# One list of 128 sums per head for the ranks above 8, sums of squares on TensorE, and new orders of work

## The reference

```python
q = (hidden_states @ Wq.T + bq).reshape(b, s, H, QD)            # H 8, QD 64
q = (q - mean) / sqrt(var + 1e-5) * ln_g + ln_b
s0 = l2norm(q[..., :32]) . l2norm(keys0)                        # 64 scores
s1 = l2norm(q[..., 32:]) . l2norm(keys1)                        # 64 scores
sc0, ix0 = top_k(s0, 16); sc1, ix1 = top_k(s1, 16)
cs = sc0[..., :, None] + sc1[..., None, :]                      # 256 cells
ci = ix0[..., :, None] + ix1[..., None, :]
fs, pos = top_k(cs, 16);  fi = ci at pos;  w = softmax(fs)
out = sum over the 16 of  gelu(x . expert_down[fi]) * w * expert_up[fi]
```

## Time and profile before

| | us |
|---|---|
| median of 3 runs (1389.09 to 1393.25) | 1392.88 |
| the profiled execution | 1389.55 |
| its span, first to last instruction | 1387.7 |
| DVE busy, share of the span | 1284.9, 93% |
| PE busy | 1029.8, 74% |
| POOL busy | 940.4, 68% |
| ACT busy | 919.2, 66% |
| mean granted clock of TensorE | 0.759 |

### The profile page before, as it was taken

How to read it: one execution, slowest core, us unless ns; L and a number is a source line. 1 busy time by engine, 2 the same in 40 slices (tenths; PEclk the granted TensorE clock), 3 DMA queues, 4 the chain that set the end, 5 groups by cost and what they waited for, 6 DMA issues and landing times.

```text
span 1387.7 us, 41186 instructions
## 1 busy us (share of the span) xinstructions
PE 1029.8 (74%) x9585; PEld 679.4 (49%) x9585; DVE 1284.9 (93%) x10050; ACT 919.2 (66%) x4155; POOL 940.4 (68%) x1947
## 2 busy tenths in 40 slices
PE   4767777877777777778778777786778878776753
PEld 2434554645455454555446454553545545463433
DVE  4349999999999989999899998999999999999995
ACT  2576867668586857858576784767658676766532
POOL 4438776786867768577677867676776777668552
PEclk7787786769788776878877696787868778685555
DMA  2100000000000000000000000000000000000000
GB/s 55 18 15 2 3 11 3 4 8 6 10 4 11 4 5 11 4 10 4 12 4 5 9 6 10 4 12 3 5 9 5 6 3 5 4 4 5 3 4 7
DMA packets 22512, 10.97 MB, mean 8 GB/s; under 512 B 13920, under 2 KB 22032, under 8 KB 22242
## 3 DMA queue, kind: packets, MB, share of 16 engines
q1 hardware_dynamic: 21618, 7.79, 2.5%
q10 hardware_dynamic: 624, 0.30, 0.1%
HBM read 4.58 MB, written 3.01 MB: 5 GB/s over the span
## 4 chain that ended last, share of the span: by engine, by line
DVE 60%; issue 15%; PE 8%; ACT 7%; POOL 6%; SPq 1%; DVEq 1%; DMA 0%; POOLq 0%; ACTq 0%
DVE idx L1466 14%; DVE val L1464 9%; DVE cr L1536 8%; DVE scores L1469 8%; DVE oh L1479 6%; DVE best L1534 4%; DVE wl L1499 3%; ACT ns_junk L863 2%; PE banks L1055 2%; DVE bns L1389 2%; DVE masked L1419 1%; POOL cs L623 1%; PE bankM L1219 1%; PE bankQ L1142 1%; ACT act_g L840 1%
## 5 line engine op out<-in xcount | busy, mean ns | idle before, releaser
L1466 DVE FIND_INDEX8 idx<-val,scores 124x8 uint16<-124x64 f32 x1536 | 304.4, 216 | 0.0
L1464 DVE MAX8 val<-scores 124x8 f32<-124x64 f32 x1536 | 210.6, 207 | 2.4 <-ACT scores L870 1.2
L1219 PE MATMUL bankM<-wl,oh 128*128 128x16 f16 x5952 | 162.8, 172 | 46.2 <-DVE wl L1499 46.2
L1219 PEld LDWEIGHTS bankM<-wl,oh 128*128 128x128 f16 x5952 | 160.0, 101 | 59.6 <-DVE wl L1499 33.2
L597 POOL TENSOR_TENSOR qscale<-nmx,power 124x16 f32<-124x16 f32 x48 | 147.8, 3079 | 45.4 <-DVE nmx L1443 45.3
L1469 DVE MATCH_REPLACE8 scores<-val,scores 124x64 f32<-124x64 f32 x768 | 151.4, 206 | 0.0
L863 ACT ACTIVATE ns_junk<-bankQ 124x32 f32<-124x32 f32 x768 | 138.0, 255 | 12.7 <-PE bankQ L1172 12.4
L1479 DVE TENSOR_SCALAR oh<-eh 128x992 f16<-128x992 int16 x384 | 135.2, 414 | 4.5 <-ACT eh L918 4.5
L863 ACT ACTIVATION_READ_ACCUMULATOR ns_junk<-bankQ 124x1 f32 x768 | 138.3, 268 | 0.0
L1108 PE MATMUL banks<-diag,probs 124*124 124x124 f32 x672 | 107.7, 327 | 25.0 <-ACT diag L808 25.0
L1227 PE MATMUL bankM<-up_x,prod 128*124 128x128 f32 x384 | 86.5, 396 | 50.5 <-DVE prod L1508 50.5
(11 more groups left out here) (196 smaller groups left out, 3067.8 us busy)
## 6 DMA issues: line engine op xcount, KB each, us to landing
x_in<-in_x SPq DMA_DIRECT2D x16, 93.8 KB
x_in<-in_x SPq DMA_DIRECT2D x16, 62.5 KB
out<-o_sb SPq DMA_DIRECT2D x16, 62.0 KB
out<-o_sb SPq DMA_DIRECT2D x16, 61.0 KB
out<-o_sb SPq DMA_DIRECT2D x16, 60.5 KB
x_in<-in_x SPq DMA_DIRECT2D x16, 31.0 KB
oh<-more SPq DMA_DIRECT2D x6, 54.0 KB
conv_w<-in_L_tok_kernel ACTq DMA_DIRECT2D x2, 128.0 KB, 3.2
```

Of the source, the lines that this page charges most:

```text
L1219: last = e.matmul(coef[:, g, :, :], oh[:, k, g, :, :].rearrange("p v t -> p (v t)"), wl[:, part, k, :, TG * g:TG * (g + 1)], start=k + par ...
L1464: last = v.max(out=v_[:, hd, s, best8], in_=src[:, hd, s, :])
L1466: last = v.max_index(out=i_[:, hd, s, best8], in_max=v_[:, hd, s, best8], in_values=src[:, hd, s, :])
```

## The change

**Ranks.** Only the first 8 of each list are ranked (`rank` steps 0 and 1; `val`, `idx`, `val_s` are half as long). Then ScalarE "lifts" the two lists of a head in place (`lift`, 16 instructions of 124x64 in a tile): every score is scaled by its own `qscale` and the best value of the other half is added. The first 8 are struck out already, so both lists hold the sums of the cells with one rank above 7. `late` (DVE) takes MAX8 over the 128 sums of a head straight into the last 8 places of `cs`, and later FIND_INDEX8. Cells are 34 + 8 = 42 in place of 50. `index_floats` (ACT) has 5 instructions in place of 1 and part 2 of `rank_sums` (POOL) 4 more, to make a place among 128 into an expert number. `scores`, `val`, `idx`, `qscale` and others have three buffers, one for each t, in place of two.

**Queries.** Both query products are computed turned (4 groups of 128x124 in place of one of 124x512). ScalarE squares all in one instruction; `q_sums` and `q_half_sums` (PE, 4 matmuls each with the squares as weights) add over partitions. `q_var` (ACT) adds the epsilon, which POOL did. `q_guard` reads its sums from `bankQ`; `bankQ` is free only when that has run on DVE (`nmx_ready`).

**Orders.** The five lists are written anew.

```diff
-                    best8 = slice(0, 8) if step < 2 else slice(8, 16)
+            def late(c, t, half, step):
+                n = c.tile(t)
+                if step == 0:
+                    dve.wait_ge(lifted, 2 * n + 1 + half)
+                    wait(dve, exp_ready, n)
+                else:
+                    dve.wait_ge(late_ready, 4 * n + 2 * half + 1)
+                for hd in range(4 * half, 4 * half + 4):
+                    both = scores[c.ring(t)][:, hd, :, :].rearrange("p s e -> p (s e)")
+                    if step == 0:
+                        last = v.max(out=cs[:, hd, INNER:NC], in_=both)
+                    else:
+                        last = v.max_index(out=late_idx[c.ring(t)][:, hd, :], in_max=cs[:, hd, INNER:NC], in_values=both)
...
+            def lift(c, t, half):
+                act.wait_ge(vals_scaled, 2 * n + 1 + half)
+                act.wait_ge(ranked, 8 * n + 4 * (half + 1))
+                for hd in range(4 * half, 4 * half + 4):
+                    for s in range(2):
+                        one = scores[c.ring(t)][:, hd, s, :]
+                        last = a.activation(one, one, ACT.Identity, scale=qscale[c.ring(t)][:, hd, s:s + 1], bias=val_s[c.ring(t)][:, hd, 1 - s, 0:1])
+                last.then_inc(lifted, 1)
...
-                for i in range(2 * H):
-                    last = a.activation(ns_junk[:, i, :], bankQ[0:NT, i * HALF:(i + 1) * HALF], ACT.Square, accum_out=nss[:, i // 2, i % 2:i % 2 + 1])
-                last.then_inc(nss_ready, 1)
+                a.activation(sqT[:, :], bankQ[:, 0:PAIRS * NT], ACT.Square).then_inc(squared2, 1)
...
-                wait(pe, nss_ready, n)
+                wait(pe, nmx_ready, n)
...
+            def q_half_sums(c, t):
+                pe.wait_ge(squared2, n + 1)
+                for k in range(PAIRS):
+                    last = e.matmul(bankQ[0:NT, 4 * k:4 * k + 4], sqT[:, k * NT:(k + 1) * NT], blocks_sb[:, 2:6], start=True, stop=True)
```

More of the change, by code:

```diff
@@ L51, in merge_matrix @@
                 m[h * NC + CELLS.index(p), h * SLOTS + s] = 1
+    for k in range(LATE):
+        for h in range(2):
+            m[h * NC + INNER + k, h * SLOTS + SLOTS - LATE + k] = 1
     assert m.sum() == 2 * NC
@@ L846, in q_squares, with q_var @@
                 act.wait_ge(q_done, n + 1)
-                wait(act, std_ready, 5 * n - 4)
-                for i in range(H):
-                    last = a.activation(sq_junk[:, i, :], bankQ[0:NT, i * QD:(i + 1) * QD], ACT.Square, scale=QD ** -0.5, accum_out=qss[:, i:i + 1])
-                last.then_inc(qss_ready, 1)
+                a.activation(sqT[:, :], bankQ[:, 0:PAIRS * NT], ACT.Square, scale=QD ** -0.5).then_inc(squared, 1)
+            def q_var(c, t):
+                n = c.tile(t)
+                act.wait_ge(qsum_done, n + 1)
+                wait(act, std_ready, 4 * n)
+                a.activation(qvar[:, :], bankQ[0:NT, 0:H], ACT.Identity, bias=eps8[:, 0:1]).then_inc(qvar_ready, 1)
             def q_stdT(c, t):
@@ L957, in body @@
                 do(q_squares, c, 2)
+                do(weight_high, c, 0)
+                do(q_var, c, 2)
+                do(lift, c, 1, 0)
                 do(p1_ln, c + 1, 1)
@@ L993, in body @@
                 do(q_gelu, c + 1, 3)
+                do(p1_probs, c + 2, 0)
+                do(index_floats, c, 2)
+                do(q_squares, c + 1, 1)
+                do(p1_diag, c + 2, 0)
+                do(best_exps, c, 2)
+                if not at(c + 1, 0):
+                    do(q_scores, c + 1, 0)
+                do(mark, c, 2)
             run(act, start, body, lambda: None)
@@ L1139, in q_inner @@
                 if low == 0:
-                    pe.wait_ge(nss_ready, 3 * b + 1)
+                    pe.wait_ge(nmx_ready, 3 * b + 1)
                 wait(pe, gelu_done, EL * b + low)
@@ L1276, in body @@
                     do(q_score, c, 0)
+                do(q_product, c, 1)
                 do(p1_scores, c + 1, 1)
-                do(q_product, c, 1)
+                do(q_sums, c, 1)
                 do(p1_turn_attn, c + 1, 0)
@@ L1618, in body @@
                 do(p1_rden, c + 1, 1)
-                do(invert_sums, c + -1, 2)
+                do(product, c + -1, 1)
                 do(p1_smax, c + 1, 2)
                 if at(c, 0):
-                    for step in range(4):
+                    for step in range(2):
                         rank(c, 0, 1, step)
-                if not at(c, 0):
-                    do(rank, c, 0, 0, 2)
-                if not at(c, 0):
-                    do(rank, c, 0, 0, 3)
                 if not at(c, 0):
@@ L1668 @@
     given += [("merge", merge_matrix()), ("identity", np.eye(128, dtype=np.float32)),
-              ("own", np.tile(np.eye(TG, dtype=np.float32), (EH, 1)))]
+              ("own", np.tile(np.eye(TG, dtype=np.float32), (EH, 1))),
+              ("blocks", np.concatenate([np.kron(np.eye(k, dtype=np.float32), np.ones((128 // k, 1), np.float32)) for k in (2, 4)], 1))]
     for name, a in given:
```

375 lines of the change are left out of this document (210 added, 165 removed).

## The result

The changed kernel takes 1495.76 us (median of 4 runs, 1485.63 to 1499.87) against 1393.07 (4 runs, 1389.09 to 1394.31) of the kernel before. The ratio is 1.0732, with a 95% interval from 1.0667 to 1.0796: slower by 7%, where 1378 was forecast. The profiled execution has a span of 1489.9 us.

The account below looks back on a forecast made before the run. The prediction took VectorE, busy 93% of the span, as the bound. From 1389.55 us it took 84 saved, added 81 of waits and took 8 back: 1378, own range 1364 to 1386, whole range 1337 to 1413.

Parts of the forecast that it names:

- VectorE's work: VectorE's ranks and `choose`: net saving of 1.76 us a tile, 84 us over 48 tiles.
- The lift: ScalarE's lift instructions: 0.34 us each, 2.7 us a group of 8, 5.4 us a tile.
- The three waits: New waits on VectorE from the new order: together 5.8 us a batch, 81 us in the run.
- Point 1: VectorE's `p1_shift` of the first norm waits for POOL's two steps: 1.5 us a batch.
- Point 3: VectorE's `late` of tile 0's second half waits for its lifts on ScalarE: 1.8 us a batch.
- Point 2: VectorE's `late` step 0 of tile 2's second half waits for ScalarE's queue: 2.5 us a batch.
- The turned products: Query products on TensorE: turning them costs nothing or a few tenths of a us either way.
- The sums: Sums of squares on TensorE: 16 new matmuls a tile at 0.135 us, 2.2 us a tile.
- I cost it at nothing: `bankQ`'s chain with `q_guard`: ScalarE's 3 us a tile given back against 2.2 for sums, so no cost.
- The cover: VectorE, 93% busy, would hide TensorE's added work, TensorE going from 63 to about 70 us of 81.
- The slower rival: Tile 2's `q_var` comes late on ScalarE, delaying the norm: 2.5 us a batch, 35 over 1378, 1413; chance 0.25.
- what is taken in: Scattered idle time in VectorE's loop that the new waits would absorb: 8 us back.

Follow-up runs that it names:

- e8: Changed kernel with one-instruction lift per half, row-shaped query products and one matmul in place of four in each sum: 1371.29 us (0.986).
- e2: Changed kernel with only the two query products back in their old row shape: 1455.95 us (1.0456).
- e6: Changed kernel with one matmul in place of four in each of the two sums of squares: 1456.58 us (1.0458).
- e5: Changed kernel with one-instruction lift per half and row-shaped query products together: 1388.69 us (0.9983).
- e3: Changed kernel with the lift of a half in one constant-scale instruction in place of 8 with per-row operands: 1425.03 us (1.0244).
- e7: Kernel before with the query half of the change alone, ranks and orders otherwise as before: 1517.15 us (1.0906).
- e13: Kernel before with both query products done twice in tile 0 alone: 1440.27 us.
- e15: Kernel before with `q_score` done twice in every tile, query products once: 1395.48 us.
- e4: Changed kernel with the first norm's `p1_shift` moved behind `finish` and the first step of `rank`: 1493.28 us (1.0697).
- e11: Kernel before with both query products done twice in all tiles: 1454.25 us.
- e9: Kernel before with the query half of the change, and tile 0's `q_guard` moved five `rank` steps up: 1519.13 us (1.0916).

## Why the prediction was wrong, point by point

- **VectorE's work: right.** 71 us less against 84, and 82 less in e8; the rates over 128 elements are as forecast.
- **The lift: right.** 0.34 us each. ScalarE's busy time is 1031, 1070 was forecast.
- **The three waits: right in place, and in size as a sum.** Point 1 is 1.25 us a batch in place of 1.5. Point 3, tile 0's second half, is 2.48 in place of 1.8, with another 1.24 ahead of the first half in some bodies. Point 2 came out smaller, 0.7 to 1.4, since VectorE was itself held up by TensorE's `experts_out` just before. Together they added 89 us against 81; that the sum fits so well is in part luck, since point 2 came out at half its size and point 3 larger.
- **The turned products: wrong, the first failed step.** "Nothing or a few tenths" came from `experts_out`, eight matmuls of a like shape. At the lower clock the first product takes 3.8 us (665.11 to 668.88) in place of 2.7, the second 2.8 in place of 2.5; at the higher, 2.2 in place of 1.4 for the first. Eight f32 weight loads stand ahead of short matmuls here, where two stood ahead of long ones. Why the first product grew more than the second, with as many loads, was not tried. e2 puts the turning at 40 us.
- **The sums: wrong in size and in what they were set against.** 16 x 0.135 = 2.2 us a tile holds at the higher clock (1.0 + 0.9); at the lower they take 1.8 each, and in tile 0 they ran there. e6 puts three quarters of them at 39 us, e8 against e5 at 17.
- **"I cost it at nothing": the step that failed.** The prediction did set up the right chain, `bankQ` with TensorE queued behind it, and then balanced averages: ScalarE gives 3 us, the sums take 2.2. It left out the longer products in the same sum, the lower clock, the hand-overs to `q_var` and `q_guard`, and the guard that is reached some 0.6 us late in 15 batches. Tile 0's way to the first `q_inner` is 1.0 us longer, not 0.8 shorter. Turned products and three quarters of the sums cost 54 us with the lifts out of the way (e3 against e8); the whole half costs 125 us in the old orders (e7). e13 shows that tile 0's way has no slack in a kernel whose VectorE is 93% busy.
- **The cover.** That VectorE's load hides TensorE's was taken from busy shares. e13 and e15 show that it holds for the scores and not for tile 0.
- **The slower rival: right sign, wrong mechanism in the main.** Its marks are there, 10.3 us at `bns` in ten waits and `qvar` with 48 us on ScalarE, and e4 shows that the norm's way has no slack. But the 1413 came from one late step; what the runs show instead is the query half (54 us) and waits of the new orders that were not taken apart.
- **The sum, by the experiments.** The prediction's own terms are 1306 with VectorE's saving whole, some 60 us for the lifts, 21 - 8 = 13 us for the first norm's wait less what is taken in, and nothing for the query half. Measured are 71 us for the lifts (e3), 54 for the query half (e3 against e8), and 65 for all that e8 keeps above 1306. Against the forecast that makes 11 + 54 + 52 = 117 of the 118 us between 1378 and 1496. So the query half at nothing is the largest single step that failed, and the 52 us are open.
- **The sum, by VectorE's waits.** The prediction had -84 + 81 - 8 = -11 on the profiled span. The profile has -71 (VectorE's work) + 89 (the two waits forecast) + 67 (the five not forecast) + 17 (spread) = +102: 1387.7 + 102 = 1490. Of the miss of 113, 13 are VectorE's work, 8 the forecast waits, and 92 the waits that were not seen, with the 8 us that were to come back.

Still open: the 65 us by which e8 misses 1306. How much of it is orders, how much the ranks' longer way over POOL and ScalarE, and how much the hand-overs and the hold of `bankQ`, which e8 keeps, was not tried.

## What to carry to other kernels

A bank or a buffer that several stages use in turn is a resource with a cycle of its own. Write its stretches down, from start to start, and look inside each for slack: does each step start as soon as the one before it ends? The stretches of any cycle add up to its period, so the sum proves nothing. Where there is no slack, as in tile 0's stretch here (51 us for 73 added), a step costs most of its length, on whichever engine; no engine's busy share covers it. Where there is slack, as around tiles 1 and 2 (32 for 92) or in another bank (6 for 78), it costs less. When work moves from one engine to another inside such a cycle, add the operation, the hand-over on both sides and the release, at that place, before setting off what the first engine gains.

## What the runs showed of the hardware

- The same first product takes 1.4 us as 128x512 with one short matmul and 2.2 as four 128x124 with four short ones at the full clock; 2.7 and 3.8 at half. Two windows, over one at half and one at full clock, show the granted clock (the value after POOL's):

```profile
665.00:669.00 4.00, 3.78 (x12) 2.40 (x12) 3.97 (x33) 0.97 (x4) 3.86 (x2) 0.50 0.00 0
...
696.00:700.00 4.00, 4.00 (x22) 2.52 (x20) 4.00 (x33) 3.83 (x16) 1.16 (x5) 1.00 0.01 4
```

- Eight matmuls with 2 or 4 columns behind 128x124 weights in f32 take 1.0 us at full and 1.8 at half clock, whether the columns are 2 or 4. The weight loads ahead of the eight that start at 662.14 are busy for 0.94 us of the 1.03, so it is they that fill the time.
- More work on TensorE did not by itself lower its mean granted clock: 0.788 in e15 and 0.779 in e11, 0.721 in e7 and 0.728 in e9, against 0.759 before. What makes the difference was not settled, and neither was what it adds to the time of e7 and e9.
